# A transformer block on one core: queries and keys of a head pair as one 1024-column tile, two small splits moved from VectorE to GpSimd, and the norms' last transpose placed later

## The reference, cut to what matters

```python
x = x + 0.5 * stack(layernorm(x))
x = x + state_space(layernorm(x))
x = x + 0.5 * stack(layernorm(x))

def stack(x):                                  # DEPTH = 6
    for i in range(DEPTH):
        x = attn_layer(shift_tokens(x), Wqkv[i], q_scale[i], k_scale[i], Wo[i]) + x
        x = ffn_layer(shift_tokens(x), ...) + x
    return x

def attn_layer(x, Wqkv, qs, ksc, Wo):          # 16 heads of 64, windows of 32 tokens
    q, k, v = split(x @ Wqkv)
    q = l2norm(q) * qs
    k = l2norm(k) * ksc
    q = q * cos * scale + rotate_half(q) * sin * scale
    k = k * cos * inv + rotate_half(k) * sin * inv
    sim = (q @ k.T) * 8, masked to the window before and the own window
    return (softmax(sim) @ v) @ Wo
```

## Time and profile before

| what | value |
|---|---|
| median of three runs | 3368.71 us (3358.27 to 3374.22) |
| profiled execution, span | 3373.6 us |
| PE busy | 2905.4 us, 86% |
| DVE busy | 2981.4 us, 88% |
| POOL busy | 2425.2 us, 72% |
| ACT busy | 2061.4 us, 61% |
| mean granted TensorE clock | 0.938 of full speed |

### The profile page before, as it was taken

How to read it: one execution, slowest core, us unless ns; L and a number is a source line. 1 busy time by engine, 2 the same in 40 slices (tenths; PEclk the granted TensorE clock), 3 DMA queues, 4 the chain that set the end, 5 groups by cost and what they waited for, 6 DMA issues and landing times. The chain is left out here.

```text
span 3373.6 us, 132100 instructions
## 1 busy us (share of the span) xinstructions
PE 2905.4 (86%) x57914; PEld 1846.3 (55%) x57914; DVE 2981.4 (88%) x4200; ACT 2061.4 (61%) x3820; POOL 2425.2 (72%) x1679
## 2 busy tenths in 40 slices
PE   5788889989989899987767788998999988999987
PEld 3455555655655555653323455565566655565653
DVE  6789899999999899896898878989999989899994
ACT  3466566666666665664764456666666666566663
POOL 3678777787787687774454667778788787787773
PEclk8899999999999999998887889999999999999998
DMA  5233332333333333320001333333343333333330
GB/s 140 65 83 73 82 91 68 89 90 72 86 92 71 84 85 71 83 72 28 7 7 44 80 72 79 75 87 86 75 97 76 90 84 72 81 94 71 86 76 14
DMA packets 114726, 250.85 MB, mean 74 GB/s; under 512 B 27244, under 2 KB 60648, under 8 KB 114152
## 3 DMA queue, kind: packets, MB, share of 16 engines
q1 hardware_dynamic: 114152, 242.40, 30.3%
HBM read 37.82 MB, written 3.15 MB: 12 GB/s over the span
## 5 line engine op out<-in xcount | busy, mean ns | idle before, releaser
L1085 ACT ACTIVATE squares<-general 128x512 f32<-128x512 f32 x768 | 453.9, 597 | 720.8 <-PE general L658 712.2
L1279 POOL TENSOR_TENSOR probs<-probs,row_sum 128x1024 f32<-128x1024 f32 x192 | 365.3, 1903 | 426.3 <-DVE row_sum L957 425.5
L1259 POOL TENSOR_TENSOR q_ring<-q_ring,partner 128x512 f32<-128x512 f32 x384 | 491.1, 1279 | 216.6 <-DMA partner<-sines 216.3
L868 DVE SCALAR_TENSOR_TENSOR sines<-general,vec,consts 128x512 f32<-128x512 f32 x768 | 560.7, 730 | 68.4 <-ACT squares L1085 65.5
L1259 POOL TENSOR_TENSOR k_ring<-k_ring,partner 128x512 f32<-128x512 f32 x384 | 490.8, 1278 | 0.0
L692 PE MATMUL general<-probs_t,v_buf 32*64 32x64 f32 x24576 | 339.4, 236 | 158.3 <-issue 87.0
L656 PE MATMUL general<-xs_hi,wqkv_lo 128*128 128x512 f32 x768 | 457.3, 595 | 15.8 <-DVE xs_lo L897 7.6
L692 PEld LDWEIGHTS general<-probs_t,v_buf 32*64 32x64 f32 x24576 | 305.6, 135 | 248.8 <-issue 241.7
L1273 POOL TENSOR_TENSOR probs<-probs,q_scale 128x1024 f32<-128x1024 f32 x192 | 365.3, 1903 | 15.1
L668 PE MATMUL general<-att,wo 128*128 128x512 f32 x768 | 370.4, 627 | 6.5 <-ACT att L1155 5.2
L719 PE MATMUL general<-k_ring,q_ring 64*32 64x64 f32 (+1 forms) x24576 | 294.2, 224 | 88.4 <-issue 53.5
(11 more groups left out here) (232 smaller groups left out, 6348.2 us busy)
## 6 DMA issues: line engine op xcount, KB each, us to landing
partner<-sines SPq DMA_DIRECT2D x1536, 128.0 KB, 2.3
wqkv_raw<-in_wqkv SPq DMA_DIRECT2D x80, 208.0 KB, 2.7
wo<-in_wo SPq DMA_DIRECT2D x12, 512.0 KB, 5.1
w<-in_w SPq DMA_DIRECT2D x12, 341.0 KB, 3.2
base_dram<-x SPq DMA_DIRECT2D x8, 256.0 KB, 2.4
att<-in_wqkv SPq DMA_DIRECT2D x2, 1024.0 KB, 6.1
sines<-base_dram SPq DMA_DIRECT2D x8, 256.0 KB, 4.0
w<-in_w SPq DMA_DIRECT2D x12, 128.0 KB
```

Of the source, the lines that this page charges most:

```text
L868: e.scalar_tensor_tensor(out=by_seq(sines[:, i % 2, which, :]), in0=g, scalar=scale, in1=both(tables[:, 2 * which + 1, :]), op0=ALU.mult, ...
L1085: e.activation(squares[:, (2 * p + which) % 4, :], general_of(("proj", k, n, p, which))[:, :], ACT.Square).then_inc(S[f"squared_{side}"], 1)
L1259: e.tensor_tensor(y, y, partner[:, i % 2, which, :], ALU.add).then_inc(S[f"rotated_{side}"], 1)
L1279: e.tensor_tensor(y, y, spread_keys(row_sum[:, i % 2, :]), ALU.mult).then_inc(S["probs_done"], 1)
```

## The change

It does six things.

1. **One tile for a pair.** `Banks.use` takes a width. The projections of queries and keys are six matmuls in a row at the start of the step, into two neighbouring banks of the ring; `q_ring` and `k_ring` become one `qk_ring` with queries and keys side by side. Square, sine, cosine and rotation are one instruction of 1024 columns each. The same for the two banks of a group's scores: one mask copy and one product with the key norms.
2. **Scaled tables.** The layer's scale is no longer an operand of each product: `dve_tables` multiplies it into the rotary tables once for each layer and stack, two instructions (24 in all), and the products are plain TENSOR_TENSORs.
3. **Norm split on GpSimd.** `pool_norms_parts` has the cast and the subtraction (before L922, L924), behind `pool_scores`.
4. **Tokens' low part on GpSimd.** `pool_split_tokens`, behind the rotation in step 6.
5. **The norms' transpose later.** `dve_norms_back` keeps the transpose only, and stands behind `dve_turn` in the odd step, no longer between the two rotations.
6. **Room.** `inv_norm` lies in `k_inv`, and `mw` and `wbc` (the scan's weights) lie in `wqkv_raw`; their three DMAs are issued when the last weights of the first stack are split, behind its last partner moves, and no longer at the start.

```diff
-    def use(self, key, sem, value):
-        at = self.next
-        self.next = (at + 1) % self.banks
-        self.of[key], self.before[key], self.filled[key] = at, self.last.get(at), self.written.get(at, False)
+    def use(self, key, sem, value, width=1):
+        at = self.next if self.next + width <= self.banks else 0
+        self.next = (at + width) % self.banks
+        taken = range(at, at + width)
+        self.of[key], self.before[key] = at, [self.last[i] for i in taken if i in self.last]
...
-                self.use(("proj", k, n, p, 0), "cos_q", (g + n) * PAIRS + p + 1)
+                self.use(("proj", k, n, p), "cos", (g + n) * PAIRS + p + 1, 2)
...
-        def pe_project(e, w, k, n, p, which):
+        def pe_project(e, w, k, n, p):
...
+            for which in range(2):
+                g, cut = two_of(("proj", k, n, p))[:, which * COLS:(which + 1) * COLS], slice(which * P, (which + 1) * P)
+                e.matmul(g, wqkv_lo[:, p, cut], xs_hi[:, r, :], start=True, stop=False)
+                e.matmul(g, wqkv_hi[:, p, cut], xs_lo[:, r, :], start=False, stop=False)
+                done = e.matmul(g, wqkv_hi[:, p, cut], xs_hi[:, r, :], start=False, stop=True)
+            done.then_inc(S["proj"], 1)
...
+        def dve_tables(e, w, k, layer):
+            w.wait_ge(S["vec_loaded"], 16)
+            w.wait_ge(S["cos"], (k * ITEMS + layer * CHUNKS) * PAIRS)
+            for which in range(2):
+                e.tensor_scalar(layer_tables[:, which, :, :], tables[:, which, :, :], vcol(layer, V_QS + which), None, ALU.mult)\
+                    .then_inc(S["tables_scaled"], 1)
...
-            e.scalar_tensor_tensor(out=by_seq(sines[:, i % 2, which, :]), in0=g, scalar=scale, in1=both(tables[:, 2 * which + 1, :]),
-                                   op0=ALU.mult, op1=ALU.mult).then_inc(S[f"sin_{side}"], 1)
+            g = by_side(two_of(("proj", k, n, p)).rearrange("p (w c) -> p w c", w=2))
+            e.tensor_tensor(by_side(sines[:, i % 2, :, :]), g, layer_table(1), ALU.mult).then_inc(S["sin"], 1)
...
-            e.scalar_tensor_tensor(out=by_seq(qk_ring[which][:, slot_of(n, p), :]), in0=g, scalar=scale,
-                                   in1=both(tables[:, 2 * which, :]), op0=ALU.mult, op1=ALU.mult).then_inc(S[f"cos_{side}"], 1)
+            e.tensor_tensor(by_side(qk_ring[:, slot_of(n, p), :, :]), g, layer_table(0), ALU.mult).then_inc(S["cos"], 1)
...
         def dve_norms_back(e, w, k, n):
-            w.wait_ge(S["k_root"], m + 1)
-            root, low, high = (norm_t[:, :, i * NORM_ROWS:(i + 1) * NORM_ROWS] for i in range(3))
-            e.tensor_copy(high.bitcast(F32R), root).then_inc(S["norms_high"], 1)
-            w.wait_ge(S["norms_high"], m + 1)
-            e.tensor_tensor(low, root, high, ALU.subtract).then_inc(S["norms_low"], 1)
             w.wait_ge(S["norms_low"], m + 1)
-            w.wait_ge(S["inv_parts"], m)
-            e.transpose(inv_norm[:, :], norm_t.rearrange("p w h -> p (w h)")).then_inc(S["k_norms_turned"], 1)
+            w.wait_ge(S["k_norms_off"], m * GROUPS)
+            e.transpose(inv_norm, norm_t.rearrange("p w h -> p (w h)")).then_inc(S["k_norms_turned"], 1)
...
-                e.tensor_tensor(cube(y), cube(general_of(("scores", k, n, group, seq))[:, :]), keys, ALU.mult).then_inc(S["k_norms_off"], 1)
+            e.tensor_tensor(cube(probs[:, i % PROBS, :]), cube(two_of(("scores", k, n, group))), keys, ALU.mult).then_inc(S["k_norms_off"], 1)
...
+            e.activation(squares[:, at:at + 2, :].rearrange("p w c -> p (w c)"), two_of(("proj", k, n, p)), ACT.Square).then_inc(S["squared"], 1)
...
+            e.tensor_tensor(y, y, partner[:, i % 2, :, :], ALU.add).then_inc(S["rotated"], 1)
+
+        def pool_norms_parts(e, w, k, n):
+            m = k * ITEMS + n
+            w.wait_ge(S["k_root"], m + 1)
+            root, low, high = (norm_t[:, :, i * NORM_ROWS:(i + 1) * NORM_ROWS] for i in range(3))
+            e.tensor_copy(high.bitcast(F32R), root).then_inc(S["norms_high"], 1)
+            w.wait_ge(S["norms_high"], m + 1)
+            e.tensor_tensor(low, root, high, ALU.subtract).then_inc(S["norms_low"], 1)
+
+        def pool_split_tokens(e, w, k, n):
+            m = k * ITEMS + n
+            w.wait_ge(S["xs_hi"], m + 1)
+            e.tensor_tensor(xs_lo[:, n % 2, :], xs[:, 1, :], xs_hi[:, n % 2, :].bitcast(F32), ALU.subtract).then_inc(S["xs_lo"], 1)
```

196 lines of the change are left out of this document (94 added, 102 removed).

## The result

The changed kernel takes 3552.45 us (median of 4 runs, 3537.86 to 3823.34; the slowest was disturbed and is left out of the ratio), beside 3370.97 us for the kernel before on the same chip. The recorded ratio is 1.0544, 95% interval 1.0501 to 1.0588. It is 5.4% slower, where 2.2% faster was forecast, and outside the range.

What follows compares the result with a forecast made beforehand. VectorE was taken as the bound, TensorE 2.7 us behind and next. An item was put between 59.0 and 61.0 us, middle 60.0 against 61.7; 46 x 1.7 = 78 us off 3373.6 gave 3295 us, range 3250 to 3341.

Steps and rivals of the forecast that it cites:

- TensorE's 54.0 us an item: TensorE's busy time, 54.03 us in a quiet item of 59.84 us, taken as the bound once VectorE is relieved.
- VectorE gives up 6.2 us an item (285 us): VectorE's relief from wider products, fewer joints and moved small operations, less table products; leaves it at 50.5 us an item.
- the joint gain per pair: On VectorE, two fewer joints a pair of 0.08 us each, so 0.32 us a pair is gained, not 476 ns.
- The small operations on GpSimd: Norm subtraction on GpSimd at its own work, 0.46 us for 128 columns, 0.9 us with the cast; upper bound 2.76.
- The walk to T + 3.7: From projection end T, square, sine, cosine and hand-overs bring the cosine at T + 3.7; values wait 4.6 us an item.
- The mask's 1.1 us: ScalarE's mask, ahead of the square, waits for the previous step's cosine: scores late by 0.7 in step 0, 0.4 in step 4.
- the friction of today's bound, 5.0: VectorE's mean item of 61.7 us less its 56.7 us busy; added to TensorE's 54.0 for the lower end, 59.0.
- the middle, 60.0: Item time taken between 59.0 us from below and 61.0 from above, 1.7 us less than 61.7.
- my own 7.0 us of new waits: TensorE's new waits an item: values 4.6, mask 1.1, spread 0.3, step 2's scores behind VectorE's transpose 1.0.
- The third: Rival: pair's chain bounds at values and step 2's spread; 3425 to 3475 us, chance 0.14; sign: values' wait above 6 us.
- Slow parts on GpSimd: Rival: norm parts on GpSimd take 5.5 us instead of 0.9, 63.9 us an item, 3475 us; chance 0.05.
- the relief passing on whole: Rival: VectorE's relief shortens the item by 4 to 6.2 us, to 3090 to 3190 us; chance 0.20.

Runs made afterwards that it cites:

- the place alone: Kernel before with the norms' cast, subtraction and transpose all still on VectorE, but behind the turn of the probabilities instead of ahead of the feed-forward sum: 1.0574.
- the half squares: Pair tile alone (the change without its moves to GpSimd, norms at their old place, 1.0674) with the square in two halves of 512 columns: 1.0481.
- that of the order: Kernel before, still in halves of 512, with the keys' projection, square and rotation right behind the queries' on four engines and in the ring: 1.0293.
- the best version: Kernel before with the norms' cast and subtraction first in GpSimd's step and the tokens' low part on GpSimd too: 0.9911, 3339.23 us.

## Why the prediction was wrong

- **What bounds the kernel.** VectorE and TensorE were named rightly, but TensorE's 54.0 us an item came from a quiet item. The mean over the stretches of the earlier trace rows is (1266.30 + 1261.75) / 46 = 55.0 us (the second stretch stands in the same view), and 55.1 after. The term was 1.0 us too small, which is 46 us of time.
- **VectorE gives up 6.2 us an item (285 us).** Measured 203.8 us. The wide products are as forecast. The 24 table products took 1631 ns each and not 740, 38.2 us against 18, and the joint gain per pair cannot be seen any more, because the sine now waits before it starts. A term that was left out altogether is larger: the 16-column operation of the variance went from 13.1 to 56.1 us in all. In the mean VectorE is no longer the bound, but in step 0 its queue still decides when the cosine is done, and this operation lies in that queue.
- **The small operations on GpSimd.** 0.29 and 0.45 us against 0.9 for both: right. The rule "Engine selection" of the Trainium skill's GPSIMD Engine Reference, twice as slow for two inputs, does not hold for these 128 columns: VectorE took 1.86 us, much of it held, for what GpSimd does in 0.45. For the 512 columns of the tokens it is 1.28 against 0.90, a factor of 1.4.
- **What TensorE waits for.** The values' wait was put at 4.6 us an item and is 256.5 / 48 = 5.3. The walk to T + 3.7 holds in steps 2, 4 and 6, and the timeline of step 2 above is its picture. By steps 0, 2, 4 and 6 the forecast was 2.0, 1.3, 0 and 1.3 us an item, and measured are 3.4, 0.9, 0.1 and 1.0. In step 0 the walk let the sine follow the square at once and had VectorE's queue wrong by over 2 us; that the total came near is in part luck, since steps 2 and 6 came 0.7 us under together. The spread's was put at 0.3 us and grew by (24.7 - 10.8) / 48 = 0.3. The mask's 1.1 us did not come, its wait (L719 before, L722 after, for ScalarE's mask) fell from 34.7 to 21.2 us. The norms' way costs little in this kernel, as the walk had it; alone, the small operations cost 3.9%.
- **The sum is the step that failed.** "From below: TensorE's 54.0 plus the friction of today's bound, 5.0", and "I take the middle, 60.0, because some of the 'issue' time falls into the new waits". Neither end of it has TensorE's own waits. TensorE already had 61.7 - 55.0 = 6.7 us of idle time an item, only 1.1 of it the wait for `q_ring`, which became part of the new one. The 2.9 us of "issue" at values and scores are still 119.8 / 48 = 2.5. Most of the rest, small waits at many lines, stayed as well. Here the engine that became the bound kept its own waits; the friction of the engine that was relieved did not take their place. By the ledger, with my own 7.0 us of new waits, less the 1.1 for `q_ring` and the 0.4 by which "issue" fell: 6.7 + 7.0 - 1.1 - 0.4 = 12.2 us idle and 55.0 + 12.2 = 67.2 us an item from above, against 10.4 and 65.5 measured. Most of the difference is the mask's 1.1 us, which did not come.
- **The rivals.** The third, the pair's chain as the bound, is nearest to what happened, at the place it named, though in step 0 the chain is not all of it. It had a chance of 0.14. It said 3475 at most and is 77 us short: 46 us of that is the quiet item's 54.0, the rest what of TensorE's own waits it left out. The sign that it named (above 6 us) was not quite reached at 5.3 either, because the point from which it decides, 7.7 us an item, was reckoned from the same 54.0 and without the waits that were there already. Reckoned with TensorE's 6.7 us of idle time, it decides as soon as new waits exceed those they take up, some 1.5 us. Slow parts on GpSimd did not happen. The same ledger speaks against the relief passing on whole: of TensorE's 6.7 us idle, only 1.1 hung on VectorE's cosine.
- **Clock.** Not forecast. It fell from 0.938 to 0.913 in the mean, with TensorE more idle, but busy time rose by 6.6 us. In the run of the place alone (0.916) busy time rose by 45.8 us of 181.8, so there it can carry at most a quarter of the loss. CLOCK is not the cause here.

Not settled is how the 1.9% behind the half squares divides between wide sine, wide cosine and the two neighbouring banks. Not tested either is how much of the loss VectorE's queue in step 0 carries, with its stretched 16-column operation: no run moves the variance's operations away from GpSimd's long ones, in the changed kernel or in that of the order. Whether an eighth bank for the ring would end the values' wait wasn't tried, since the sums have it.

## What to carry to other kernels

Before a change relieves the busiest engine, write down the next engine's ledger, busy time plus each named wait, as a mean over the steady part. Do not let the old waits go unless you can name what ends them sooner, and add the new ones to them. Walk the new chain through every kind of step, with what stands in each engine's queue ahead of it, and not only through the step where the queues are empty. Halves that interleave on several engines, and share a ring of banks, are cover: merging them saved fixed costs on an engine that no longer counted in the mean, and lengthened the time until the banks were free. A small operation that moves to another engine goes by its place in that engine's queue; ahead of two long instructions it gained 0.4%, behind them it lost 2.2%.

## What the hardware showed unexpectedly

A small scalar operation of VectorE between SBUF tiles was stretched by GpSimd. L847, 16 columns wide, takes 1002 ns in the mean over 56 calls (181 to 1883), and the same operation took 234 ns before:

```profile
L846 DVE TENSOR_SCALAR norm_t<-norm_t 128x16 f32<-128x16 f32 x56 | 13.1, 234 | 1.9
```

One of them in the changed kernel, with the GpSimd instruction beside it:

```profile
1115.47 1.90 POOL L1292 TENSOR_TENSOR probs<-probs,q_scale 128x1024 f32<-128x1024 f32 x1
1115.61 1.80 DVE L847 TENSOR_SCALAR norm_t<-norm_t 128x16 f32<-128x16 f32 x1
1117.33 2.35 POOL L1265 TENSOR_TENSOR qk_ring<-qk_ring,partner 128x1024 f32<-128x1024 f32 x1
```

It began 0.14 us after GpSimd's instruction and ended 0.04 us after it. 37 of the 56 calls take over 0.5 us, and 36 of them end 0.03 to 0.05 us behind a GpSimd instruction that had begun before them. With one SBUF input only, it is held as the two-input subtraction of the earlier trace rows was. The Trainium skill, SBUF - State Buffer, "Who interferes with whom", names `tensor_scalar` among the operations that can take the shared pair, under conditions on its operands, and the trace agrees. How long it is held depends on when it falls: in the best version, with GpSimd busier, it takes 359 ns, and with the keys right behind the queries, all in halves, 1319. The 24 table products (474 to 2572 ns for 512 columns, mean 1631) run beside GpSimd too, except at the start of a stack, where GpSimd is idle and two of them take 0.87 us.
